# A mixer kernel on one core: the zero test of the attention scores moves from VectorE to two ScalarE passes

## The chip, the core and the metric

The kernel runs on one core of a Trainium2 chip. The metric is the device time of one launch in microseconds (us); lower is better. TensorE is PE in the rows below, VectorE is DVE, ScalarE is ACT, GpSimd is POOL, and SyncE is SP.

## What is computed

The reference is a chain of residual blocks over 16 sequences of 512 tokens of width 128: a mixture of experts, causal attention, the mixture again, and then two more mixtures around a state-space scan. Only the attention matters here:

```python
q = jnp.einsum('bse,ke->bsk', x, WQ)
k = jnp.einsum('bse,ke->bsk', x, WK)
v = jnp.einsum('bse,ve->bsv', x, WV)
scores = jnp.einsum('bsk,btk->bst', q, k) * SCALE
masked = jnp.where(jnp.tril(scores) == 0, -jnp.inf, scores)
attn = jax.nn.softmax(masked, axis=-1)
return jnp.einsum('bst,btv->bsv', attn, v)
```

A score is masked when it lies above the diagonal, and also when it is exactly zero.

## The kernel before, in words

The kernel is a row of stages with a barrier between them. The change is in `attention_stage`, whose tiles are named `att_...` in the rows. It keeps all tokens of all sequences in the resident tile `X`, and works through the 16 sequences s = 0 to 15 in order. Each sequence is cut into four row tiles i = 0 to 3 of 128 queries. Row tile i sees n = (i + 1) * 128 keys, so its scores are 128 x n, and there are 64 row tiles in all. `psS`, `hole`, `S`, `E`, `psE` and `PT` have two buffers each, taken in turn by row tiles.

For a row tile, PE writes the scores to `psS` and adds the causal triangle with a third matmul (L1046). DVE then makes `hole`, which is -1e30 where the score is exactly zero (L1248), adds it to the scores and takes the row maximum in one custom instruction (L1252), and scales the maximum into `ntop` (L1254, signal `topped`). ACT takes the exponential (L1178, signal `exped`). PE transposes it into `psE`, ACT copies that to `PT` (L1169), PE multiplies it with V into `psO`, and DVE divides and adds it to `X` (L1259, L1261; these two are `finish`).

Every engine has its own fixed program order, written out by hand, and the engines are tied by counting semaphores. PE runs one row tile ahead: its body for row tile i begins with the scores of i + 1. Between the row tiles stand the projections of the next sequence. ACT evicts K after row tile 1 (`att_KT`, L1156), then Q (`att_QT`, L1158), and V after row tile 2 (`att_V`, L1162). After that it normalizes the sequence after next (`att_xn`, L1147, four instructions), and evicts its transpose after row tile 3 (`att_xnT`, L1152).

The stage also routes its output to the experts of the next stage, for a pair of sequences at a time, and for one at a time at the end (s = 12 to 15). These are the tiles `att_r_...`. ACT normalizes them (`att_r_xn`, L246), PE transposes and multiplies, ACT evicts (`att_r_xnT`, L326) and takes an exponential (`att_r_prob`, L407), DVE picks the experts and writes the row numbers `att_r_idx` (L451), and POOL scatters the rows with one indirect DMA for 128 rows (L471). `att_r_xn` is a ring of two, so a group's normalized rows wait for the scatters of the group two before.

On DVE small pieces of routing and statistics work are woven into the gaps. `small.under(part)` runs one step of them at each point where `part` yields, and `chain.link` yields once after it has issued its instruction.

Of the kernel before, what the change touches and what calls it, by code (L numbers as in the profile page):

```python
# [15 lines left out]
ALU = mybir.AluOpType  # L16
ACT = mybir.ActivationFunctionType
AX = mybir.AxisListType

P = 128  # L20
# [24 lines left out]
EPS = 1e-5  # L45
NEG = -1e30
SCALE = D ** -0.5
INNER, STATES, RANK, TAPS = 256, 16, 64, 4
DT = INNER // P
PAD = 2 * (TAPS - 1)  # L50
# [714 lines left out]
def load_stage(nc, k, x, here, consts, l0_bg, gate_w, gamma, beta):  # L765


    with Stage(nc, "load") as st:
        loaded, zeroed, cleared = map(st.sem, ("loaded", "zeroed", "cleared"))
        empty = st.sb("empty", [P, SPREAD * ROW])  # L770
        token_i, slot_i = st.sb("token_i", [P, TILES], I32), st.sb("slot_i", [P, SPREAD], I32)
        raw = st.sb("raw", [P, 3 * P])
        counted = st.sem("counted")
        block = st.block()

        @block.gpsimd
        def _(pool):
            nc.gpsimd.iota(token_i[:, :], pattern=[[TOPK * P, TILES]], base=0, channel_multiplier=TOPK)
            nc.gpsimd.iota(slot_i[:, :], pattern=[[1, SPREAD]], base=0, channel_multiplier=SPREAD).then_inc(counted, 1)

        @block.sync
        def _(sp):
            wide = lambda v: v.rearrange("(a e) -> a e", a=1)
            for dst, src in ((raw[:, :], consts[:, P:4 * P]), (k.ident[:, :], consts[:, 0:P]), (k.small[:, :], consts[:, 36 * P:]),
                             (k.bg[:, :], wide(l0_bg).to_broadcast([P, EXPERTS])), (k.gamma[:, :], gamma.rearrange("(p a) -> p a", a=1)),
                             (k.beta[:, :], beta.rearrange("(p a) -> p a", a=1)), (k.gate_w[:, 0, :], gate_w[0]), (k.gate_w[:, 1, :], gate_w[1])):
                sp.dma_start(dst, src).then_inc(loaded, 16)
            for s in range(2):
                load_rows(sp, k, x, here, s)
            sp.wait_ge(loaded, 8 * 16)  # L790

        @block.scalar
        def _(act):
            act.wait_ge(cleared, 1)
            act.dma_start(k.xslots[DUMP:DUMP + BLOCK, :].rearrange("(p r) d -> p (r d)", p=P), empty[:, :]).then_inc(zeroed, 16)
            act.wait_ge(zeroed, 16)

        @block.vector
        def _(dve):
            nc.vector.memset(k.ones[:, :], 1.0)  # L800
            clear_rows(nc, empty[:, :]).then_inc(cleared, 1)
            dve.wait_ge(counted, 1)
            nc.vector.tensor_copy(k.token[:, :], token_i[:, :])
            nc.vector.tensor_copy(k.slot[:, :], slot_i[:, :])
            dve.wait_ge(loaded, 8 * 16)
            nc.vector.tensor_copy(k.before[:, :], raw[:, 0:P])
            nc.vector.tensor_copy(k.causal[:, :], raw[:, P:2 * P])
            nc.vector.tensor_copy(k.ident_bf[:, :], raw[:, 2 * P:3 * P])


# [150 lines left out]
def attention_stage(nc, k, wqkv, source):  # L961


    with Stage(nc, "att") as st:
        sem, sb, pb = st.sem, st.sb, st.pb
        w_ready, linked, normed, flipped, turned, q_summed, k_summed, v_summed, qk_ready, v_ready = map(
            sem, ("w_ready", "linked", "normed", "flipped", "turned", "q_summed", "k_summed", "v_summed", "qk_ready", "v_ready"))
        scored, topped, exped, p_flipped, p_turned, summed, added, holed, cleared = map(
            sem, ("scored", "topped", "exped", "p_flipped", "p_turned", "summed", "added", "holed", "cleared"))
        W = sb("W", [P, 3, P])  # L970
        xn = sb("xn", [P, 4, D])
        xnT = sb("xnT", [P, SEQ])
        QT, KT = sb("QT", [P, 2, SEQ]), sb("KT", [P, 2, SEQ])
        V = sb("V", [P, 2, 4, D])
        hole, S, E, PT = (sb(n, [P, 2, SEQ]) for n in ("hole", "S", "E", "PT"))
        top, ntop, total, inv = (sb(n, [P, SEQ_TILES]) for n in ("top", "ntop", "total", "inv"))
        empty = sb("empty", [P, SPREAD * ROW])
        psT = pb("psT", [P, SEQ])
        psQ, psO = pb("psQ", [P, SEQ]), pb("psO", [P, D])
        psS, psE = pb("psS", [P, 2, SEQ]), pb("psE", [P, 2, SEQ])  # L980
# [11 lines left out]
        there = lambda s: 0 <= s < BATCH  # L992
        block = st.block()
        ST = SEQ_TILES
# [144 lines left out]
        def _(act):  # L1139
# [10 lines left out]
            def turn_rows(s):  # L1150
                act.wait_ge(flipped, s + 1)
                nc.scalar.activation(xnT[:, :], psT[:, :], ACT.Copy).then_inc(turned, 1)  # L1152

            def project_qk(s, b):
                act.wait_ge(k_summed, s + 1)
                nc.scalar.activation(KT[:, b, :], psT[:, :], ACT.Copy).then_inc(qk_ready, 1)  # L1156
                act.wait_ge(q_summed, s + 1)
                nc.scalar.activation(QT[:, b, :], psQ[:, :], ACT.Copy).then_inc(qk_ready, 1)  # L1158

            def project_v(s, b):  # L1160
                act.wait_ge(v_summed, s + 1)
                nc.scalar.activation(V[:, b, :, :], psQ[:, :].rearrange("p (a d) -> p a d", a=4), ACT.Copy).then_inc(v_ready, 1)  # L1162

            def turn_p(s, i):
                t, n = s * ST + i, (i + 1) * P
# [5 lines left out]
            def body(s, b):  # L1171
                due, fresh = ends.get(s - 2), ends.get(s - 1)
                for i in range(ST):
                    t, n = s * ST + i, (i + 1) * P
                    act.wait_ge(topped, t + 1)
                    if t > 1:
                        act.wait_ge(p_flipped, t - 1)
                    nc.scalar.activation(E[:, i % 2, 0:n], S[:, i % 2, 0:n], ACT.Exp, bias=ntop[:, i:i + 1], scale=SCALE,  # L1178
                                         accum_out=total[:, i:i + 1]).then_inc(exped, 1)
                    if i > 0:  # L1180
                        turn_p(s, i - 1)
# [33 lines left out]
            N.act_root(nc, act, 1)  # L1215
            normal(1)
            turn_rows(1)
            for s in range(BATCH):
                body(s, s % 2)
            s, b, g = BATCH - 1, 1, len(pairs) - 1  # L1220
# [9 lines left out]
        def _(dve):  # L1230
            chain = Chain(dve, linked)
# [11 lines left out]

            def mask(s, i):
                t, n, h = s * ST + i, (i + 1) * P, i % 2
                dve.wait_ge(scored, t + 1)

                yield from chain.link(nc.vector.tensor_scalar(hole[:, h, 0:n], psS[:, h, 0:n], 0.0, NEG, ALU.is_equal, ALU.mult))  # L1248
                if t > 1:
                    dve.wait_ge(exped, t - 1)  # L1250
                dve.sem_inc(holed, 1)
                yield from chain.link(nc.vector.tensor_tensor_reduce(out=S[:, h, 0:n], in0=psS[:, h, 0:n], in1=hole[:, h, 0:n], scale=1.0, scalar=3.0 * NEG,  # L1252
                                                                     op0=ALU.add, op1=ALU.max, accum_out=top[:, i:i + 1]))
                nc.vector.tensor_scalar(ntop[:, i:i + 1], top[:, i:i + 1], -SCALE, None, ALU.mult).then_inc(topped, 1)  # L1254

            def finish(s, i):
                t = s * ST + i
# [62 lines left out]
            s, g = BATCH - 1, len(pairs) - 1  # L1320
# [637 lines left out]
```

## Time and profile before

| | |
|---|---|
| time of 3 runs, median (lowest to highest) | 3136.72 us (3132.16 to 3138.05) |
| the profiled execution: own time | 3140.43 us |
| the profiled execution: span of its instructions | 3138.6 us |
| PE busy | 2462.0 us (78%) |
| DVE busy | 2072.7 us (66%) |
| ACT busy | 1591.6 us (51%) |
| POOL busy | 1698.8 us (54%) |

The profiled execution's own time lies 1.8 us above its span. The busy shares are averages over all stages with different limits, so they say little about the attention stage. That stage stands between about 484 and 798 us of the span.

### The profile page before, as it was taken

How to read it: one execution, taken by the hardware profiler on the slowest of the kernel's cores; microseconds unless marked ns; L12 is line 12 of the kernel's file. 1: busy time of each engine (PE TensorE's matmuls, PEld its weight loads, DVE VectorE, ACT ScalarE, POOL GpSimd, SP SyncE). 2: the span in 40 equal slices, each digit the busy share in tenths (PEclk: the TensorE clock that was granted, in tenths of full speed). 3: DMA queues.
4: the chain of work that ended last, by engine and by line, in shares of the span. 5: the costliest groups of instructions: out<-in, count | busy, mean ns of one | idle time of the engine just before them, and what ended most of it. 6: DMA issues, size and time to landing. Idle time of an engine off the chain costs nothing. (4 is left out here: it accounts for less than half of the span.)

```text
span 3138.6 us, 49074 instructions
## 1 busy us (share of the span) xinstructions
PE 2462.0 (78%) x12952; PEld 1742.6 (56%) x12952; DVE 2072.7 (66%) x6083; ACT 1591.6 (51%) x3093; POOL 1698.8 (54%) x1349
## 2 busy tenths in 40 slices
PE   4239995884799754399978888888988898759991
PEld 4239994663799633399933333333433343349991
DVE  6414445775344455155539999999999999955553
ACT  3115554672455443255546666656666666425550
POOL 5745550455355347555515567666666667645551
PEclk9999998996899966699989999999999999879995
DMA  9147771211677532477724344434334344237775
GB/s 329 53 131 229 226 224 58 69 53 41 205 228 226 159 99 78 131 229 226 216 75 142 129 134 143 140 124 136 136 124 133 135 136 145 102 114 228 226 227 170
DMA packets 268819, 479.26 MB, mean 153 GB/s; under 512 B 37453, under 2 KB 181803, under 8 KB 268560
## 3 DMA queue, kind: packets, MB, share of 16 engines
q1 hardware_dynamic: 225280, 405.41, 42.4%
q0 software_dynamic: 34816, 68.00, 6.0%
q10 hardware_dynamic: 8592, 4.33, 0.5%
q8 instruction: 54, 0.88, 0.1%
q14 instruction: 77, 0.63, 0.1%
HBM read 383.22 MB, written 98.54 MB: 153 GB/s over the span
## 5 line engine op out<-in xcount | busy, mean ns | idle before, releaser
L1731 POOL TENSOR_TENSOR ssm_HC<-ssm_H,ssm_BC 128x1024 f32<-128x1024 f32 x255 | 599.4, 2351 | 416.3 <-DVE ssm_psX L1801 329.3
L1492 PE MATMUL ssm_psY<-ssm_HC,ident 128*128 128x512 f32 x1020 | 516.9, 634 | 94.0 <-POOL ssm_HC L1731 93.8
L1650 ACT ACTIVATE ssm_dA<-ssm_delta,A 128x511 f32<-128x511 f32 x512 | 332.9, 710 | 194.0 <-DVE ssm_H L1810 133.9
L1492 PEld LDWEIGHTS ssm_psY<-ssm_HC,ident 128*128 128x128 f32 x1020 | 192.6, 198 | 363.6 <-issue 201.4
L1808 DVE TENSOR_TENSOR_SCAN ssm_H<-ssm_dA,ssm_psX 128x512 f32<-128x512 f32 x256 | 309.7, 1210 | 0.0
L1810 DVE TENSOR_TENSOR_SCAN ssm_H<-ssm_dA,ssm_psX 128x512 f32<-128x512 f32 x256 | 305.4, 1193 | 0.0
L471 POOL DMA_INDIRECT xslots<-att_r_xn,att_r_idx x128 | 128.3, 1002 | 176.6 <-DVE att_r_idx L451 138.5
L877 POOL DMA_INDIRECT b_back<-b_yr,b_to_row x144 | 139.8, 971 | 151.2 <-DVE b_yr L952 129.3
L877 POOL DMA_INDIRECT a_back<-a_yr,a_to_row x144 | 139.8, 971 | 150.4 <-DVE a_yr L952 128.4
L877 POOL DMA_INDIRECT d_back<-d_yr,d_to_row x144 | 139.8, 971 | 147.9 <-DVE d_yr L952 126.0
L877 POOL DMA_INDIRECT c_back<-c_yr,c_to_row x144 | 139.8, 971 | 143.1 <-DVE c_yr L952 119.3
L921 ACT ACTIVATE b_H<-b_psH,b_W 128x256 f32<-128x256 f32 x288 | 127.4, 473 | 125.6 <-PE b_psH L898 125.6
L921 ACT ACTIVATE d_H<-d_psH,d_W 128x256 f32<-128x256 f32 x288 | 127.4, 473 | 125.3 <-PE d_psH L898 125.3
L921 ACT ACTIVATE a_H<-a_psH,a_W 128x256 f32<-128x256 f32 x288 | 127.4, 473 | 124.4 <-PE a_psH L898 124.4
L921 ACT ACTIVATE c_H<-c_psH,c_W 128x256 f32<-128x256 f32 x288 | 127.4, 473 | 123.9 <-PE c_psH L898 123.9
L921 ACT ACT_TABLE_LOAD x72 | 92.4, 1283 | 183.4 <-PEq L162 182.2
L471 POOL DMA_INDIRECT xslots<-ssm_r_xn,ssm_r_idx x128 | 160.1, 1251 | 34.1 <-issue 23.7
L1801 DVE TENSOR_TENSOR ssm_psX<-ssm_ux,ssm_BC 128x512 f32<-128x512 f32 x256 | 176.4, 689 | 0.0
L471 POOL DMA_INDIRECT xslots<-to_c_r_xn,to_c_r_idx x128 | 125.7, 982 | 91.1 <-DVE to_c_r_idx L451 51.1
L1796 DVE TENSOR_TENSOR ssm_psX<-ssm_ux,ssm_BC 128x512 f32<-128x512 f32 x256 | 174.0, 680 | 0.6
L1428 PE MATMUL ssm_psA<-ssm_hT,Wtap 128*128 128x512 f32 x360 | 165.4, 603 | 5.4 <-ACT ssm_hT L1586 5.1
L471 POOL DMA_INDIRECT xslots<-to_a_r_xn,to_a_r_idx x128 | 125.5, 981 | 66.4 <-issue 41.0
(566 smaller groups left out, 5817.6 us busy)
## 6 DMA issues: line engine op xcount, KB each, us to landing
ssm_BC<-bc_rows SPq DMA_DIRECT2D x128, 1024.0 KB, 5.5
a_W<-in_l_pack SPq DMA_DIRECT2D x72, 514.0 KB, 3.4
b_W<-in_l_pack SPq DMA_DIRECT2D x72, 514.0 KB, 3.3
c_W<-in_l_pack SPq DMA_DIRECT2D x72, 514.0 KB, 3.4
d_W<-in_l_pack SPq DMA_DIRECT2D x72, 514.0 KB, 3.4
a_xs<-xslots SPq DMA_DIRECT2D x72, 131.0 KB
b_xs<-xslots SPq DMA_DIRECT2D x72, 131.0 KB
c_xs<-xslots SPq DMA_DIRECT2D x72, 131.0 KB
```

What stands on the lines that cost most here:

```text
L471: pool.indirect_dma_start(out=self.k.xslots[:, :], out_offset=bass.IndirectOffsetOnAxis(ap=self.ids(s, b)[:, i:i + 1].bitcast(U32), axis=0 ...
L877: pool.indirect_dma_start(out=target[:, :], out_offset=bass.IndirectOffsetOnAxis(ap=to_row[:, q, s:s + 1].bitcast(U32), axis=0), in_=yr[:, ...
L921: nc.scalar.activation(H[:, b, f, :], psH[:, f, 0:BLOCK], gelu, bias=W[:, q, HIDDEN + FT * D + f:HIDDEN + FT * D + f + 1]).then_inc(h_read ...
L1428: last = nc.tensor.matmul(out, Wtap[:, c, t, dt * P:(dt + 1) * P], hT[:, PAD - back:PAD - back + SEQ], start=(t == 0), stop=(t == TAPS - 1))
L1492: last = nc.tensor.matmul(psY[:, dt, :], k.ident[:, :], HC[:, n % RP, dt, :], start=(n == 0), stop=(n == NB - 1))
L1650: last = nc.scalar.activation(dA[:, n % RA, dt, 1:], delta[:, b, dt, 1:], ACT.Exp, scale=A[:, dt, n:n + 1])
L1731: nc.gpsimd.tensor_tensor(HC[:, n % RP, :, :], H[:, n % RH, :, :], BC[:, n // CHUNK % SLOTS, 1, n % CHUNK:n % CHUNK + 1, :].to_broadcast([ ...
L1796: nc.vector.tensor_tensor(psX[:, 0, :], ux[:, 0, :], BC[:, c % SLOTS, 0, n % CHUNK, :], ALU.mult).then_inc(dBx_half, 1)
L1801: nc.vector.tensor_tensor(psX[:, 1, :], ux[:, 1, :], BC[:, c % SLOTS, 0, n % CHUNK, :], ALU.mult).then_inc(dBx_done, 1)
L1808: nc.vector.tensor_tensor_scan(H[:, n % RH, 0, :], dA[:, n % RA, 0, :], psX[:, 0, :], 0.0, ALU.mult, ALU.add).then_inc(h_half, 1)
L1810: nc.vector.tensor_tensor_scan(H[:, n % RH, 1, :], dA[:, n % RA, 1, :], psX[:, 1, :], 0.0, ALU.mult, ALU.add).then_inc(h_ready, 1)
```

## The change

`hole` is now made by ACT, in two passes: `|score * 1e36|`, and then `max(0, 1 - that)`, which is 1 for an exact zero and 0 otherwise. For this the queries carry a factor of -2^-50, so that a hole of 1 is large against any score. DVE waits for `holed` in place of `scored`, and its custom instruction negates the sum. The exponential and `ntop` have the factor taken back in their scales. The causal constant is 1 in place of -1e30; it is made once, in the first stage.

ACT makes the holes of row tile i + 1 ahead of the exponential of row tile i. DVE's `mask` has one `chain.link` less, so it steps the woven work once less for each row tile.

```diff
+SHRINK = 2.0 ** -50
...
-            nc.vector.tensor_copy(k.causal[:, :], raw[:, P:2 * P])
+            nc.vector.tensor_scalar(k.causal[:, :], raw[:, P:2 * P], 1.0 / NEG, None, ALU.mult)
...
-                nc.scalar.activation(QT[:, b, :], psQ[:, :], ACT.Copy).then_inc(qk_ready, 1)
+                nc.scalar.activation(QT[:, b, :], psQ[:, :], ACT.Copy, scale=-SHRINK).then_inc(qk_ready, 1)
...
+            def holes(s, i):
+
+                t, n, h = s * ST + i, (i + 1) * P, i % 2
+                act.wait_ge(scored, t + 1)
+                nc.scalar.activation(hole[:, h, 0:n], psS[:, h, 0:n], ACT.Abs, scale=1e36).then_inc(distant, 1)
+                act.wait_ge(distant, t + 1)
+                nc.scalar.activation(hole[:, h, 0:n], hole[:, h, 0:n], ACT.Relu, scale=-1.0, bias=1.0).then_inc(holed, 1)
...
                 for i in range(ST):
                     t, n = s * ST + i, (i + 1) * P
+                    if t > 0:
+                        act.wait_ge(topped, t)
+                    if i + 1 < ST:
+                        holes(s, i + 1)
+                    elif there(s + 1):
+                        holes(s + 1, 0)
                     act.wait_ge(topped, t + 1)
                     if t > 1:
                         act.wait_ge(p_flipped, t - 1)
-                    nc.scalar.activation(E[:, i % 2, 0:n], S[:, i % 2, 0:n], ACT.Exp, bias=ntop[:, i:i + 1], scale=SCALE,
+                    nc.scalar.activation(E[:, i % 2, 0:n], S[:, i % 2, 0:n], ACT.Exp, bias=ntop[:, i:i + 1], scale=SCALE / SHRINK,
                                          accum_out=total[:, i:i + 1]).then_inc(exped, 1)
...
+            holes(0, 0)
...
-                dve.wait_ge(scored, t + 1)
-
-                yield from chain.link(nc.vector.tensor_scalar(hole[:, h, 0:n], psS[:, h, 0:n], 0.0, NEG, ALU.is_equal, ALU.mult))
+                dve.wait_ge(holed, t + 1)
                 if t > 1:
                     dve.wait_ge(exped, t - 1)
-                dve.sem_inc(holed, 1)
-                yield from chain.link(nc.vector.tensor_tensor_reduce(out=S[:, h, 0:n], in0=psS[:, h, 0:n], in1=hole[:, h, 0:n], scale=1.0, scalar=3.0 * NEG,
+                dve.sem_inc(begun, 1)
+                yield from chain.link(nc.vector.tensor_tensor_reduce(out=S[:, h, 0:n], in0=psS[:, h, 0:n], in1=hole[:, h, 0:n], scale=-1.0, scalar=3.0 * NEG,
                                                                      op0=ALU.add, op1=ALU.max, accum_out=top[:, i:i + 1]))
-                nc.vector.tensor_scalar(ntop[:, i:i + 1], top[:, i:i + 1], -SCALE, None, ALU.mult).then_inc(topped, 1)
+                nc.vector.tensor_scalar(ntop[:, i:i + 1], top[:, i:i + 1], -SCALE / SHRINK, None, ALU.mult).then_inc(topped, 1)
```

ACT's program in the middle of an odd sequence, from the exponential of row tile 1 on. Before:

```order
L1178 ACTIVATE att_E,att_total<-att_S,att_ntop 128x256
L1169 ACTIVATE att_PT<-att_psE 128x128
L326 ACTIVATE att_r_xnT<-att_psQ 128x512
L1156 ACTIVATE att_KT<-att_psT 128x512
L1158 ACTIVATE att_QT<-att_psQ 128x512
L1178 ACTIVATE att_E,att_total<-att_S,att_ntop 128x384
```

And of the change, the same place:

```order
L1169 ACTIVATE att_hole<-att_psS 128x384
L1171 ACTIVATE att_hole<-att_hole 128x384
L1193 ACTIVATE att_E,att_total<-att_S,att_ntop 128x256
L1178 ACTIVATE att_PT<-att_psE 128x128
L327 ACTIVATE att_r_xnT<-att_psQ 128x512
L1157 ACTIVATE att_KT<-att_psT 128x512
L1159 ACTIVATE att_QT<-att_psQ 128x512
L1169 ACTIVATE att_hole<-att_psS 128x512
L1171 ACTIVATE att_hole<-att_hole 128x512
L1193 ACTIVATE att_E,att_total<-att_S,att_ntop 128x384
```

Two instructions have come in ahead of every exponential, and nothing else has moved. The number of table loads in ACT's program is the same, 72.

DVE's program in an even sequence, between the scores of row tile 2 and those of row tile 3 (128x512). `att_n_shift` ends the statistics that ACT's `att_xn` waits for, and `att_r_pos` waits for PE's routing matmuls. Before:

```order
L1252 ISA att_S,att_top<-att_psS,att_hole 128x384
L1252 ISA att_top 128x1
L234 SCALAR_TENSOR_TENSOR att_n_rstd<-att_n_newton,att_n_root 128x8
L211 TENSOR_SCALAR att_r_mean<-att_r_mean 128x8
L212 SCALAR_TENSOR_TENSOR att_r_odd<-att_r_odd 128x8
L1254 TENSOR_SCALAR att_ntop<-att_top 128x1
L239 SCALAR_TENSOR_TENSOR att_n_shift<-att_n_mean,att_n_rstd 128x8
L213 SCALAR_TENSOR_TENSOR att_r_var<-att_r_var,att_r_odd 128x8
L447 TENSOR_TENSOR att_r_pos<-att_psR,att_r_run 128x128
```

And of the change, the same place:

```order
L1266 ISA att_S,att_top<-att_psS,att_hole 128x384
L1266 ISA att_top 128x1
L234 TENSOR_TENSOR att_n_newton<-att_n_newton,att_n_shifted 128x8
L209 TENSOR_TENSOR att_r_mean<-att_r_stats 128x8
L210 TENSOR_TENSOR att_r_var<-att_r_stats 128x8
L211 TENSOR_TENSOR att_r_odd<-att_r_stats 128x8
L1268 TENSOR_SCALAR att_ntop<-att_top 128x1
L235 SCALAR_TENSOR_TENSOR att_n_rstd<-att_n_newton,att_n_root 128x8
L212 TENSOR_SCALAR att_r_mean<-att_r_mean 128x8
L213 SCALAR_TENSOR_TENSOR att_r_odd<-att_r_odd 128x8
L448 TENSOR_TENSOR att_r_pos<-att_psR,att_r_run 128x128
L240 SCALAR_TENSOR_TENSOR att_n_shift<-att_n_mean,att_n_rstd 128x8
```

With one yield less, the woven statistics are one step behind: `att_n_shift` stood ahead of `att_r_pos` and now stands behind it.

## Rows read from the trace of the kernel before

**Rows 1.** Stretches (start:end, length): engines' busy us (instructions), PEclk, DMA share, GB/s.

```profile
510.00:546.39 36.39, 29.52 (x176) 22.82 (x177) 27.26 (x123) 21.46 (x64) 0.00 (x0) 0.92 0.19 59
631.92:659.99 28.07, 23.73 (x196) 19.08 (x196) 22.00 (x117) 20.06 (x56) 16.44 (x17) 1.00 0.26 77
```

**Rows 2.** Who waited for whom, 500 to 760: total, times, longest.

```profile
ACT att_E L1178 <- DVE att_ntop L1254: 51.5, 37, 4.4
```

**Rows 3.** ACT's timeline, one pair: start, length, [idle before <-releaser].

```profile
631.92 0.72 ACT L1178 ACTIVATE att_E<-att_S,att_ntop 128x512 f32<-128x512 f32 x1 [0.83 <-DVE att_ntop L1254]
...
635.02 0.39 ACT L1178 ACTIVATE att_E<-att_S,att_ntop 128x128 f32<-128x128 f32 x1
...
636.43 1.64 ACT L246 ACTIVATE att_r_xn<-X,att_r_shift,att_r_rstd 128x128 f32<-128x128 f32 x4
...
642.38 0.60 ACT L1158 ACTIVATE att_QT<-att_psQ 128x512 f32<-128x512 f32 x1 [1.16 <-PE att_psQ L1028]
643.15 0.61 ACT L1178 ACTIVATE att_E<-att_S,att_ntop 128x384 f32<-128x384 f32 x1 [0.17 <-DVE att_ntop L1254]
...
648.04 0.72 ACT L1178 ACTIVATE att_E<-att_S,att_ntop 128x512 f32<-128x512 f32 x1 [1.12 <-DVE att_ntop L1254]
...
650.67 0.20 ACT L223 ACTIVATE att_n_root<-att_n_shifted 128x8 f32<-128x8 f32 x1
650.90 0.21 ACT L225 ACTIVATE att_n_root<-att_n_root 128x8 f32<-128x8 f32 x1
...
655.83 0.61 ACT L1178 ACTIVATE att_E<-att_S,att_ntop 128x384 f32<-128x384 f32 x1 [1.49 <-DVE att_ntop L1254]
...
659.99 0.72 ACT L1178 ACTIVATE att_E<-att_S,att_ntop 128x512 f32<-128x512 f32 x1 [0.83 <-DVE att_ntop L1254]
```

**Rows 4.** DVE's and PE's timelines in that pair.

```profile
658.17 0.68 DVE L1248 TENSOR_SCALAR att_hole<-att_psS 128x512 f32<-128x512 f32 x1
...
659.07 0.69 DVE L1252 CUSTOM_DVE_ANT_0 att_S<-att_psS,att_hole 128x512 f32<-128x512 f32 x1
...
642.18 0.81 PE L1044 MATMUL att_psS<-att_KT,att_QT 128*128 128x384 f32 x2
...
643.04 0.22 PE L1046 MATMUL att_psS<-causal,ident_bf 128*128 128x128 bf16 x1
```

**Rows 5.** ACT groups by shape, 480 to 790: busy, mean ns | idle before.

```profile
L246 ACT ACTIVATE att_r_xn<-X,att_r_shift,att_r_rstd 128x128 f32<-128x128 f32 x64 | 26.3, 484 | 9.8 <-DMA xslots<-att_r_xn,att_r_idx 6.9 <-DVE att_r_shift L239 2.9
...
L1169 ACT ACTIVATE att_PT<-att_psE 128x512 f32<-128x512 f32 x16 | 9.3, 580 | 0.0
...
L1178 ACT ACTIVATE att_E<-att_S,att_ntop 128x128 f32<-128x128 f32 x16 | 6.3, 395 | 0.4
...
L1169 ACT ACTIVATE att_PT<-att_psE 128x128 f32<-128x128 f32 x16 | 4.1, 257 | 0.5 <-PE att_psE L1052 0.5
```

**Rows 6.** The same view of the scan stage.

```profile
L1632 ACT ACTIVATE ssm_pre<-ssm_psA,col 128x512 f32<-128x512 f32 x31 | 21.2, 682 | 23.3 <-PE ssm_psA L1466 23.3
...
L1637 ACT ACTIVATE ssm_rest<-ssm_pre 128x1024 f32<-128x1024 f32 x16 | 16.9, 1057 | 0.5
```

**Rows 7.** ACT's timeline at the stage's start.

```profile
525.04 0.39 ACT L1178 ACTIVATE att_E<-att_S,att_ntop 128x128 f32<-128x128 f32 x1
...
529.89 0.51 ACT L1178 ACTIVATE att_E<-att_S,att_ntop 128x256 f32<-128x256 f32 x1 [3.89 <-DVE att_ntop L1254]
...
535.15 0.71 ACT L1178 ACTIVATE att_E<-att_S,att_ntop 128x512 f32<-128x512 f32 x1
...
546.39 0.71 ACT L1178 ACTIVATE att_E<-att_S,att_ntop 128x512 f32<-128x512 f32 x1
```

**Rows 8.** ACT's and POOL's timelines at its end.

```profile
710.66 1.65 ACT L246 ACTIVATE att_r_xn<-X,att_r_shift,att_r_rstd 128x128 f32<-128x128 f32 x4 [0.52 <-DMA xslots<-att_r_xn,att_r_idx]
...
733.19 1.65 ACT L246 ACTIVATE att_r_xn<-X,att_r_shift,att_r_rstd 128x128 f32<-128x128 f32 x4 [6.38 <-DMA xslots<-att_r_xn,att_r_idx]
...
689.13 0.97 POOL L471 DMA_INDIRECT xslots<-att_r_xn,att_r_idx  x1 [8.82 <-DVE att_r_idx L451]
```

More of the change, by code:

```diff
@@ L967, in attention_stage @@
             sem, ("w_ready", "linked", "normed", "flipped", "turned", "q_summed", "k_summed", "v_summed", "qk_ready", "v_ready"))
-        scored, topped, exped, p_flipped, p_turned, summed, added, holed, cleared = map(
-            sem, ("scored", "topped", "exped", "p_flipped", "p_turned", "summed", "added", "holed", "cleared"))
+        scored, topped, exped, distant, begun, p_flipped, p_turned, summed, added, holed, cleared = map(
+            sem, ("scored", "topped", "exped", "distant", "begun", "p_flipped", "p_turned", "summed", "added", "holed", "cleared"))
         W = sb("W", [P, 3, P])
```

## Prediction

> **What bounds the kernel now.** The change lies in the attention stage alone, so the page's shares say nothing, and I read the stage by stretches first. From 631.92 to 659.99, one pair of sequences, PE is busy 23.7 of 28.1 us, DVE 22.0 and ACT 20.1 [rows 1]. No engine is full: they take turns in waiting. The list of waits says for whom: ACT waited 51.5 us, 37 times, for DVE's `ntop` before the exponential [rows 2]. That looks like room on ACT, and like a VectorE on the path. So the question is where on ACT's timeline this room is, since ACT's order is fixed. It is in lumps: 0.83 and 1.12 us ahead of row tile 3, 1.49 ahead of row tile 2 of the even sequence [rows 3]. From 631.92 to the end of `att_r_xn` at 638.07 ACT has next to none: the exponential at 635.02 starts without a wait [rows 3]. At the stage's end ACT waits for scatters: the wait of 6.38 us at 733.19 [rows 8].
>
> **What is removed.** 64 DVE passes. Of a 512-wide row tile the pass starts at 658.17 and the custom instruction at 659.07 [rows 4], so its `ntop` can come 0.90 us earlier, if the holes are there.
>
> **What is added: the price of a pass.** Neither pass is in the trace in its form. Abs from PSUM: below, the copy `att_PT`, 0.257 us for 128 and 0.580 for 512; above, `ssm_pre` L1632, which also reads a bias column, 0.682 for 512 [rows 5, 6]. I take 0.27 to 0.59, near the copy, since the new pass has no column. Relu from SBUF: L1637 is an affine with constants only, 1.057 us for 1024 [rows 6]; the copies' slope is 0.108 us per 128 [rows 5], which gives 0.63 for 512 and 0.30 for 128. Above it lies the exponential, 0.395 for 128, which reads a column [rows 5]. The second pass waits for the first on the same engine, like the pair at 650.67 and 650.90: a start 0.03 us after the end of the first [rows 3]. An instruction that doesn't wait overlaps its forerunner by 0.10: the four of `att_r_xn` at 636.43 last 1.64 together, and one lasts 0.484 [rows 3, 5]. Two passes thus take 0.51, 0.72, 0.93 and 1.16 us for row tiles 0 to 3: **3.32 us a sequence**. By the bounds it is 3.06 (two copies) to 4.03 (both with a column).
>
> The Trainium skill, page "ScalarE: Activation LUTs", section "What ACT_TABLE_LOAD costs", gives 186 ns + 0.833 ns an element for constants, 93 ns more for each column and 93 ns of overlap. The rows above bear it out (0.63 here, 0.61 by the rule); by it an estimate is 3.37 us a sequence, 0.6 us more in the whole sum.
>
> **Where the passes land: a pair.** I go along ACT's order from the exponential of row tile 3 at 631.92 to the one at 659.99 [rows 3], with each start at the later of ACT's and its giver's.
> - Odd half. ACT's 3.1 us to 635.02 stay. Then come passes for row tile 1 (0.72) with nothing to hide in, so the second half of `att_r_xn` ends 0.72 late, at 638.8. Passes for row tile 2 (0.93) take the place of a wait. PE transposes that `att_r_xn` and has K and Q behind it, so Q's scores come 0.75 late too. QT starts at 643.1 (before 642.38), still after a wait of 1.15. The passes for row tile 3 need their scores, which PE needs 1.08 us for after Q (642.18 to 643.26, [rows 4]): a wait of 0.42 behind QT's 0.5, then 1.16. The exponential of row tile 2 goes from 643.15 to 645.2. V, `att_r_prob` and `att_xn` follow 1.3 to 1.5 late. DVE's routing waits for `att_r_prob`, so of its 0.90 gained, 0.6 are lost: `ntop` at 648.5. ACT gets there at 648.2 and, after 0.51 of passes, starts row tile 3 at 648.7, where it was 648.04.
> - Even half. 0.72 + 0.93 + 1.16 + 0.51 us of passes. The waits they could fill are those for `ntop`, 0.88, 1.49 and 0.83, and what is left are short waits for PE (0.12, 0.25, 0.40), since K, Q and the scores of row tile 3 now start from an ACT that is late with `att_PT`.
> - `att_n_shift` now stands behind `att_r_pos` in DVE's program, so `att_xn` waits another 0.33 for PE's routing matmuls.
>
> Sum: start to start ACT's own work in the pair is 19.4 us (its busy 20.06 [rows 1] less the overlaps). Add 6.64 of passes and the waits left: 0.57 for K, 1.15 and 0.42, and 0.12 + 0.25 + 0.40 + 0.33, together 3.2. 19.4 + 6.6 + 3.2 = 29.2 us where it was 28.07: **+1.15 us a pair**. ACT is now what the pair lasts; what is late next is PE, behind `att_PT` and the exponential.
>
> **The start.** Sequences 0 to 2 carry no routing on ACT, and it is busy 21.5 of 36.4 us [rows 1]. The first holes wait for `att_xnT`, so the exponential at 525.04 comes 3.9 late. The wait of 3.89 at 529.89, for DVE's sums and statistics [rows 7], swallows 3 of it, for DVE's new order puts this `ntop` only 0.35 later. From there ACT is full: the exponential of row tile 3 at 535.15 comes 3.15 late and the one at 546.39 **4.0** late (a sequence of 11.24 us becomes 12.1: some 10.6 of work and passes and 1.2 to 1.5 of waits for K, Q and scores).
>
> **The end.** From the scatters that begin at 689.13 on [rows 8], 16 DMAs and the free ring buffer set `att_r_xn` at 710.66, and the next 16 that at 733.19. Lateness that ACT adds in between fits into the waits of 0.52 and 6.38. Five pairs lie between 546.39 and there: 5 x 1.15 = 5.75. After 733.19 DVE is the late one again: the passes cost 0.45, the last removed pass gives back 0.90, so -0.45.
>
> The causal constant, the scale on QT and the scaled `ntop` are the same instructions with other numbers: nothing. Total: 4.0 + 5.75 - 0.45 = **+9.3 us**. The profiled execution took 3140.43 us (span 3138.6, 1.8 around it), so its like would take 3149.7; it lies 3.7 above the median of the runs, and against 3136.72 the forecast is **3146.0 us**, +0.30%.
>
> **The rivals.**
> - *Hidden.* ACT's 51.5 us of waiting [rows 2] take up nearly all of 16 x 3.3 = 53 us, and the rest is noise: 3137 us. For it: the waits are of the right size and ahead of the right instruction. Against: they lie in the wrong half, and some turn into waits for PE.
> - *The path through DVE gets shorter (faster).* If the passes fit, row tile 3's `ntop` comes 0.90 earlier in both halves, and PE's next scores and `att_xnT` with it: 5 x 1.8 = 9, so 3128 us. It decides whether ACT has 0.5 us free ahead of row tile 3 after its `att_xn`. In the trace it idles there 1.12 and 0.83 [rows 3]; but V comes late by the passes of row tile 3, which eat that.
> - *Dearer passes or a lower clock (slower still).* With the upper prices a sequence has 0.7 us more, over 13 sequences 9: 3155 us. Likewise the granted clock: 1.00 with PE busy 85% of a pair, 0.92 at the start with 81% [rows 1], so there it fell from the 2.4 GHz level part of the time. A pair of 29.2 us has PE at 81%. If that brings 0.92, PE's 23.7 us become 25.8, at most 2 us a pair on top, so 3156 us.
>
> **How the numbers follow.** I give my sum 0.62, hidden 0.20, faster 0.08 and dearer 0.10. The sum's own range is 3140 to 3152: lower prices take 13 x 0.26 = 3.4 off, and waits left out come on top. A measurement of this kernel tells about 0.2%, 6.3 us, from no change; my sum lies 3 us over that, so I count 0.54 of its 0.62 as slower. Slower 0.64, same 0.20 + 0.08 = 0.28, faster 0.08. The range takes in "hidden" and most of the dearer case: 3136 to 3157.
>
> **What would show it.** Right: a pair lasts 29 to 29.5 us, ACT busy 26 or more of them; its waits for `ntop` fall from 51.5 to under 15 us, while those for K, Q and scores grow; the exponential that was at 546.39 is 4 us later; a 512-wide Abs takes 0.57 to 0.62 and a Relu 0.61 to 0.65. The stage's length up to the next stage's first matmul grows by some 9 us, and the other stages keep theirs. Wrong: passes of 0.7 us; a pair of 28 us with ACT still waiting for `ntop` (then PE or DVE was the bound and ACT had room); or a start that costs nothing, since the wait of 3.89 us there swallows all.

## The result, and the profile after

The changed kernel took 3142.07 us (median of 20 runs, 3138.2 to 3148.98), the kernel before on the same chip 3135.77 (20 runs, 3130.06 to 3141.29). The ratio is 1.0023, with a 95% interval of 1.0017 to 1.0029: slower by 0.23%, 6.3 us. A second comparison on another chip gave 3144.19 against 3135.07, ratio 1.0030 [1.0018, 1.0042], 9.1 us. The profiled execution after has a time of its own of 3141.97 us and a span of 3140.2.

The spans of the two profiled executions differ by 1.6 us only, so the first thing to do is to cut them at the stage. I cut from the table load that opens the attention stage on ACT (488.31 before, 489.09 after) to the first matmul of the next stage (800.86 and 811.07). Kernel before, both parts by windows:

```profile
488.31:800.86 312.55, 206.21 (x1536) 165.38 (x1537) 202.40 (x1040) 164.83 (x450) 128.28 (x128) 0.83 0.20 60
800.86:3138.60 2337.74, 1931.00 (x9016) 1274.16 (x9016) 1649.66 (x4086) 1234.83 (x2234) 1304.73 (x943) 0.91 0.50 157
```

And after:

```profile
489.09:811.07 321.98, 213.75 (x1536) 169.62 (x1536) 175.02 (x976) 212.24 (x578) 125.41 (x128) 0.83 0.20 58
811.07:3140.20 2329.13, 1920.64 (x9016) 1268.80 (x9016) 1649.32 (x4086) 1234.75 (x2234) 1304.89 (x943) 0.92 0.51 157
```

The stage grew by 9.43 us. The rest has the same instructions and was 8.6 us shorter, with PE busy 10 us less at a slightly higher granted clock: the profiled execution of before happened to lie 4.7 us above its own median. Only the stage tells of the change. In it ACT has 128 instructions and 47.4 us more, DVE 64 instructions and 27.4 us less.

Stretches of the stage after, the start and then a pair; they answer to [rows 1]:

```profile
512.50:552.48 39.98, 33.22 (x180) 24.86 (x179) 23.89 (x119) 31.29 (x88) 0.00 (x0) 0.85 0.20 53
581.69:610.90 29.21, 24.07 (x198) 19.15 (x197) 18.52 (x108) 25.80 (x73) 15.62 (x17) 1.00 0.25 74
```

ACT's busy time in a pair went from 20.1 to 25.8 us, a little under the 26 that the prediction named as its sign, and the pair from 28.07 to 29.21. DVE is now busy 18.5. The list of waits, 500 to 770, against [rows 2]:

```profile
DVE X L1275 <- PE att_psO L1065: 31.4, 27, 6.9
...
DVE att_S L1266 <- ACT att_hole L1171: 17.1, 15, 4.2
ACT att_QT L1159 <- PE att_psQ L1029: 10.1, 15, 1.2
ACT att_hole L1169 <- PE att_psS L1047: 8.8, 17, 2.0
ACT att_E L1193 <- DVE att_ntop L1268: 8.2, 3, 3.2
ACT att_KT L1157 <- PE att_psT L1024: 7.5, 14, 2.2
```

The roles are turned round: ACT's 51.5 us of waiting for `ntop` are down to 8.2, all three of them at the stage's end, and DVE waits for ACT's holes and for PE's `psO`, which needs ACT's exponentials and `PT`. The waits for K and Q did not grow, as the prediction had it: they were 9.6 and 9.9 before. New are those for the scores, 8.8. ACT's timeline of the pair answers to [rows 3]:

```profile
581.69 0.71 ACT L1193 ACTIVATE att_E<-att_S,att_ntop 128x512 f32<-128x512 f32 x1
...
591.05 0.60 ACT L1157 ACTIVATE att_KT<-att_psT 128x512 f32<-128x512 f32 x1 [0.50 <-PE att_psT L1024]
592.80 0.60 ACT L1159 ACTIVATE att_QT<-att_psQ 128x512 f32<-128x512 f32 x1 [1.15 <-PE att_psQ L1029]
593.78 0.60 ACT L1169 ACTIVATE att_hole<-att_psS 128x512 f32<-128x512 f32 x1 [0.39 <-PE att_psS L1047]
594.41 0.63 ACT L1171 ACTIVATE att_hole<-att_hole 128x512 f32<-128x512 f32 x1
...
598.48 0.71 ACT L1193 ACTIVATE att_E<-att_S,att_ntop 128x512 f32<-128x512 f32 x1
...
603.83 0.60 ACT L1157 ACTIVATE att_KT<-att_psT 128x512 f32<-128x512 f32 x1 [0.18 <-PE att_psT L1024]
604.69 0.60 ACT L1159 ACTIVATE att_QT<-att_psQ 128x512 f32<-128x512 f32 x1 [0.26 <-PE att_psQ L1029]
605.67 0.60 ACT L1169 ACTIVATE att_hole<-att_psS 128x512 f32<-128x512 f32 x1 [0.39 <-PE att_psS L1047]
...
608.50 1.65 ACT L1148 ACTIVATE att_xn<-X,att_n_shift,att_n_rstd 128x128 f32<-128x128 f32 x4 [0.22 <-DVE att_n_shift L240]
...
610.90 0.71 ACT L1193 ACTIVATE att_E<-att_S,att_ntop 128x512 f32<-128x512 f32 x1
```

These seven rows with a bracket are all of ACT's waits in 29.21 us, 3.09 us together. The odd half takes 16.79 us where it took 16.12, the even half 12.42 where it took 11.95. The price of a pass, in the view of [rows 5]:

```profile
L1171 ACT ACTIVATE att_hole<-att_hole 128x512 f32<-128x512 f32 x16 | 10.1, 630 | 0.5
L1169 ACT ACTIVATE att_hole<-att_psS 128x512 f32<-128x512 f32 x16 | 9.6, 598 | 7.4 <-PE att_psS L1047 7.4
...
L1171 ACT ACTIVATE att_hole<-att_hole 128x128 f32<-128x128 f32 x16 | 5.0, 310 | 0.5
L1169 ACT ACTIVATE att_hole<-att_psS 128x128 f32<-128x128 f32 x16 | 4.2, 261 | 0.0
```

The end of the stage, against [rows 8]:

```profile
743.69 1.65 ACT L247 ACTIVATE att_r_xn<-X,att_r_shift,att_r_rstd 128x128 f32<-128x128 f32 x4 [6.20 <-DMA xslots<-att_r_xn,att_r_idx]
```

From the table load this `att_r_xn` is at 254.60 where it was at 244.88: 9.72 us late, of which 9.43 reach the next stage.

### The profile page after: what moved, and what is told of

Read it like the earlier page. It is cut to its first block and busy times, and to the rows that moved or that the text cites. A ratio compares the mean times of both kernels' runs of the same rounds, so it can differ in the third digit from the quotient of the medians.

```text
span 3140.2 us, 49200 instructions
## 1 busy us (share of the span) xinstructions
PE 2460.2 (78%) x12952; PEld 1742.2 (55%) x12952; DVE 2044.7 (65%) x6019; ACT 1638.9 (52%) x3221; POOL 1696.0 (54%) x1349
```

## The experiments

All medians below stand beside runs of the kernel before on the same chip. "A pair" is the time from the 512-wide exponential of one even sequence to that of the next even one; the pair with routing begins with s = 2. The experiments ran on three chips.

**The first chip was no good for this.** On it the kernel before took 3278.32 us, 4.5% more than elsewhere, and every kernel's pair was near 40 us. Most of it lies in the attention stage: in the version with the relief alone it takes 415.33 us there and 303.35 on the second chip, 112 of the 154 us between the two medians. DVE's and ACT's timelines of that version there, `e1_relief`:

```profile
621.87 0.60 ACT L326 ACTIVATE att_r_xnT<-att_psQ 128x512 f32<-128x512 f32 x1 [5.23 <-remote]
...
633.11 0.23 DVE L399 TENSOR_TENSOR att_r_L<-att_psR,bg 128x64 f32<-128x64 f32 x1 [12.81 <-remote]
633.15 0.60 ACT L1158 ACTIVATE att_QT<-att_psQ 128x512 f32<-128x512 f32 x1 [6.45 <-DMA a_xs<-xslots]
```

ACT stands for 5 to 6 us ahead of an eviction, and the transfer named, of another stage's tile, is nothing that the eviction depends on. Such waits come in every pair but the first, and the stage's start is 40 us longer too. They swallow or add microseconds at will, so I read from this chip only the first pair, and put all four of its questions again on the others. Why that chip stands there is left open.

### Only the relief: DVE's pass removed, nothing added

The kernel before without DVE's zero test. `hole` is cleared once, so exact zeros aren't masked. With the line goes its step of woven work, so DVE has the order of the change here too, `att_n_shift` behind `att_r_pos`.

```diff
+            chain(nc.vector.memset(hole[:, :, :], 0.0))
...
-                yield from chain.link(nc.vector.tensor_scalar(hole[:, h, 0:n], psS[:, h, 0:n], 0.0, NEG, ALU.is_equal, ALU.mult))
```

> The kernel before without DVE's zero pass and without any ACT pass: the hole tile is zeroed once, so only the causal triangle masks and exact zeros are not looked for. It measures what the relief of DVE is worth by itself. Theory A (ACT's passes cost what DVE's relief gives and more): row tile 3's ntop comes 0.9 us earlier in both halves of a pair, so a pair of 28.07 us takes 26.3 to 27.3, and the kernel is 5 to 11 us faster than before. Rival B (DVE's pass was never on the path): a pair of 28.0 us, the time of before within 2 us.

> The kernel before without DVE's zero pass and without an ACT pass, as in the first call (the hole tile is zeroed once, so only the causal triangle masks), to see its time where the stage has no stalls. In the first call its first pair took 26.88 us where before takes 28.06, but the later ones 38 to 42 with stalls in them. Theory A: without stalls 27.0 us a pair and 6 to 11 us faster than before. Rival B: within 2 us of before.

Measured: on the first chip 3280.68 against 3278.32, ratio 1.0011 [0.9996, 1.0027], with a first pair of 26.88. On the second 3126.39 against 3135.07, ratio 0.9965 [0.9951, 0.9978], 8.7 us faster; the stage takes 303.35 us. A pair there:

```profile
600.40:627.00 26.60, 22.95 (x198) 19.02 (x197) 18.26 (x107) 19.92 (x57) 15.87 (x16) 1.00 0.27 82
```

So DVE's path did set part of the time: 1.47 us a pair, with the changed order in it. The pair of 27.0 that was expected is undercut by 0.4. The change had that to gain.

### Only the cost: two more passes on ACT, DVE's kept

The passes read `KT` and write a tile that nobody uses; they stand and wait where the change's do.

```diff
+            def holes(s, i):
+
+                t, n, h = s * ST + i, (i + 1) * P, i % 2
+                act.wait_ge(scored, t + 1)
+                nc.scalar.activation(extra[:, h, 0:n], KT[:, s % 2, 0:n], ACT.Abs, scale=1e36).then_inc(distant, 1)
+                act.wait_ge(distant, t + 1)
+                nc.scalar.activation(extra[:, h, 0:n], extra[:, h, 0:n], ACT.Relu, scale=-1.0, bias=1.0).then_inc(passed, 1)
```

> The kernel before with its DVE zero pass kept, and ACT's two passes added at the places of the change, with the same wait for the scores, but reading the K tile from SBUF and writing a tile that nobody reads. It measures the passes' cost without DVE's relief and without DVE waiting for ACT. Theory A: ACT's own time is the cost, so a pair takes 29.2 to 30.2 us and the kernel is 9 to 16 us slower than before. Rival B (the passes fit into ACT's waits, and the cost of the change is DVE waiting for the holes): a pair of 28.1 to 28.5 us, at most 3 us slower than before.

> The kernel before with two more ScalarE passes per row tile, of the same lengths and at the same places as in the change, but with KT for a source and an unused tile for a target; DVE's zero test stays, and its order too. Theory (the cost of the change is ScalarE's work, its relief is DVE's pass gone): both costs and no relief, a pair of 30.8 us and 14 to 22 us slower than before, so 8 to 14 us slower than the change. Rival (the wait of DVE on ACT's holes is what costs, and ScalarE's own work is hidden in its 51.5 us of waiting): a pair of 28.1 to 28.6 and at most 3 us slower than before.

Measured: on the first chip ratio 1.0053 [1.0038, 1.0068], first pair 30.77. On the third 3151.11 against 3134.6, ratio 1.0050 [1.0035, 1.0064], 16.5 us slower, the stage 328.04 us, pairs of 30.1 to 30.5 where 30.8 was expected. The first, with a granted clock of 0.94, is below; the one pair at 1.00 takes 30.13.

```profile
552.41:582.50 30.09, 25.43 (x196) 20.01 (x194) 21.68 (x114) 26.19 (x73) 0.20 (x1) 0.94 0.13 36
```

ACT's passes alone cost 16.5 us, although ACT waited 51.5 us before. With the relief of 8.7 they make 7.8, and the change measured 6.3 and 9.1. But the intervals of these two ratios are some 4 us wide to either side, so that sum can't exclude a third term, and the stage in the profiles shows one. There the relief gives 9.20 us and the passes cost 15.49, together 6.3, where the change costs 9.43 and 9.95. In a pair at a clock of 1.00 the two make 2.06 less 1.47, 0.59 us, and the change costs 1.14. So on top of ACT's passes DVE's relief gives back less than by itself, 0.92 us (30.13 to 29.21). What takes the rest, DVE's waits for the holes or an ACT that has no room for an earlier `ntop`, no run separates. The row for `KT` shows something by the way, shown at the end.

### Half the cost: one pass on ACT

The changed kernel with one pass per row tile. It leaves out the test for zero, so its holes aren't holes.

```diff
-                nc.scalar.activation(hole[:, h, 0:n], psS[:, h, 0:n], ACT.Abs, scale=1e36).then_inc(distant, 1)
-                act.wait_ge(distant, t + 1)
-                nc.scalar.activation(hole[:, h, 0:n], hole[:, h, 0:n], ACT.Relu, scale=-1.0, bias=1.0).then_inc(holed, 1)
+                nc.scalar.activation(hole[:, h, 0:n], psS[:, h, 0:n], ACT.Relu, scale=1e-30).then_inc(holed, 1)
```

> The changed kernel with only one ACT pass for a row tile (a Relu of the scores times 1e-30, so the hole tile is practically zero and only the causal triangle masks). It halves the suspected cost. Theory A (ACT's passes set the pair): 3.3 us a pair less of ACT work, of which the waits for PE and DVE take back some: a pair of 27.0 to 27.8 us, 7 to 11 us faster than the change and 0 to 4 faster than before. Rival B (the order of waits, holes before the exponential, is what costs and not the passes' length): a pair of 28.7 us or more, at most 3 us faster than the change.

> The changed kernel with one ScalarE pass in place of the two (the Relu of the scores times 1e-30 straight from PSUM; it leaves out the test for zero, so its holes aren't holes). The order on DVE is that of the change, and the passes for row tiles 0 to 3 take 0.31 to 0.63 us, half of the two. Again on a chip where the attention stage doesn't stand still. Theory (the length of ACT's work in a pair makes the change slower, and what DVE is relieved of comes out as soon as ACT's work is short enough): a pair of 27.1 to 27.3 us (before 28.07), 0 to 6 us faster than before. Rival (DVE's order, with att_n_shift behind att_r_pos, costs time whatever ACT does): a pair of 28.3 or more, slower than before.

Measured: on the first chip ratio 1.0049 [1.0033, 1.0064], which is worth little there; its first pair is 27.15. On the third 3127.35 against 3134.6, ratio 0.9982 [0.9973, 0.9991]: faster by 7.2 us, a little more than the 0 to 6 expected; its stage is 5.0 us shorter than before. All five pairs take 27.13 us. Windows, and ACT's timeline in a pair:

```profile
657.13:684.26 27.13, 23.16 (x198) 19.07 (x197) 18.35 (x108) 22.25 (x64) 16.07 (x16) 1.00 0.13 41
```

```profile
638.91 0.60 ACT L1157 ACTIVATE att_KT<-att_psT 128x512 f32<-128x512 f32 x1 [1.06 <-PE att_psT L1024]
...
650.40 0.60 ACT L1157 ACTIVATE att_KT<-att_psT 128x512 f32<-128x512 f32 x1 [0.64 <-PE att_psT L1024]
...
655.08 1.65 ACT L1148 ACTIVATE att_xn<-X,att_n_shift,att_n_rstd 128x128 f32<-128x128 f32 x4 [0.89 <-DVE att_n_shift L240]
```

The pair shrinks by 2.08 us for 3.55 us less of ACT's busy time. So ACT's second pass is what turns the gain of DVE's relief into a loss. At half the price ACT no longer sets the pair alone: its waits for PE and for `att_n_shift` make 4.77 us in place of 3.09. The first pass costs little, 0.53 us against the 26.60 with the relief alone.

### The order on DVE: one more step of woven work

The changed kernel with `yield` once more in `mask`, ahead of the wait for `holed`, so that `att_n_shift` stands ahead of `att_r_pos` again.

```diff
+                yield
                 dve.wait_ge(holed, t + 1)
```

> The changed kernel with one more yield in mask, ahead of its wait, so that the woven work steps as often as before and att_n_shift stands ahead of att_r_pos again. Theory A with its 0.33 us a pair for att_n_shift: 28.9 us a pair, 1.5 to 2.5 us faster than the change. Rival B (the step is free, or the statistics that now stand between the custom instruction and ntop cost as much): the time of the change within 1 us, a pair of 29.2.

> The changed kernel with one more step of woven work per row tile, so that DVE's order is again that of before (att_n_shift ahead of att_r_pos). Theory by the prediction's term (att_xn waits 0.33 us a pair longer by that order): a pair of 28.9 us, 1.5 us less in the stage. Rival (on the full ACT this wait is swallowed by another): a pair of 29.2 to 29.4, and the time that of the change, 3142 to 3144 where before is 3136, within 1 us.

Measured: on the first chip ratio 1.0059 [1.0043, 1.0075]. On the third 3142.92 against 3134.6, ratio 1.0027 [1.0018, 1.0037], the stage 321.52 us. The wait of 0.22 ahead of `att_xn` is gone:

```profile
695.71 1.64 ACT L1148 ACTIVATE att_xn<-X,att_n_shift,att_n_rstd 128x128 f32<-128x128 f32 x4
```

This pair, from 669.09 to 698.10, takes 29.01 us: its even half 12.10 in place of 12.42, its odd half 16.91 in place of 16.79. The other pairs take 29.36, 29.76 (with a granted clock of 0.94), 29.14 and 29.08, so against 29.21 the gain is 0.2 us in the best pair and none in the first. The stage is 0.5 to 1 us shorter (321.98 and 322.50 in the two profiles of the changed kernel), but these have one and two pairs at a lower clock, and the whole can't be told from the changed kernel. So the order costs at most 0.2 us a pair on the full ACT, not the 0.33 of the theory.

### Passes only where ACT waited

Three kernels give ACT a part of the row tiles and leave DVE the others, with the new scales everywhere. The condition is `by_act`.

```diff
+        by_act = lambda s, i: s % 2 == 0 and i == 3
...
+                if by_act(s, i):
+                    dve.wait_ge(holed, held(s, i))
+                else:
+                    dve.wait_ge(scored, t + 1)
+                    yield from chain.link(nc.vector.tensor_scalar(hole[:, h, 0:n], psS[:, h, 0:n], 0.0, 1.0, ALU.is_equal, ALU.mult))
```

Row tile 3 of the even sequences:

> A mixture: ACT makes the holes only for row tile 3 of even sequences, where the kernel before had ACT waiting 1.49 us ahead of the exponential of row tile 2; DVE makes all others, as before. Theory A (what counts is whether a pass finds ACT idle): the passes of 1.16 us fit, ntop of that row tile comes up to 0.9 us earlier, a pair of 27.2 to 28.0 us, and 2 to 6 us faster than before. Rival B (any ACT pass delays): a pair of 28.5 us or more and 1 to 4 us slower than before.

Row tile 3 of all sequences, `i == 3`:

> The same with row tile 3 of every sequence on ACT. In the odd half the passes wait for scores that PE finishes only after Q's, and they stand ahead of V, whose lateness reaches DVE's routing. Theory A: that half gives back what the even half gains, a pair of 27.8 to 28.6 us, and -3 to +2 us against before. Rival B: a pair of 29 us or more, 5 us slower than before.

Row tiles 2 and 3 of the even sequences, `s % 2 == 0 and i > 1`:

> ScalarE makes the holes of row tiles 2 and 3 of the even sequences alone, where it waited 1.49 and 0.83 us for DVE's ntop; DVE makes the other 48. Against the version with row tile 3 of the even sequences alone, which had a pair of 27.17 and was 3.5 us faster than before. Theory (a pass is free only where ACT waits for DVE): the 0.93 us for row tile 2 fit into the 0.88 us ahead of its forerunner's exponential, so a pair of 27.1 to 27.3 and 2 to 6 us faster than before. Rival (ACT is already the bound in that version, so any pass adds its length): a pair of 28.0 us, equal to before within 2 us.

And the changed kernel again, beside the first two of them:

> The changed kernel again, on another chip than the first result, to have its trace beside the experiments. Theory A: a pair of 29.2 us as before, and +0.2 to +0.3% against the kernel before, if this chip has no stalls of its own. Rival C (the chip on which the first four experiments ran holds engines back while they wait for nothing in the program, and there more instructions cost more than their time): where such stalls show, +0.4 to +0.6%.

| holes made by ACT | us against before | ratio | load to E(2,3) | pair | stage |
|---|---|---|---|---|---|
| none (before, profiled) | | | 58.08 | 28.07 | 312.55 |
| even, row tile 3 | 3131.61 against 3135.07 | 0.9986 [0.9977, 0.9995] | 59.97 | 27.17 | 309.36 |
| all, row tile 3 | 3133.04 against 3135.07 | 0.9988 [0.9979, 0.9997] | 60.30 | 27.13 | 309.28 |
| even, row tiles 2 and 3 | 3133.47 against 3134.6 | 0.9997 [0.9988, 1.0006] | 60.72 | 27.52 | 312.08 |
| all (the change, again) | 3144.19 against 3135.07 | 1.0030 [1.0018, 1.0042] | 63.09 | 29.22 | 322.50 |

E(2,3) is the exponential of row tile 3 of sequence 2. The pair is the undisturbed one of the five: the second version has one of 28.65 besides, the last one of 30.07, one of 30.08 and one of 29.34. In the row of before the stage has two pairs of 29.39 at a clock of 0.94 in it, 2.6 us above five pairs of 28.07.

ACT's timeline of the first version, in the even half, shows how a pass goes for nothing; compare the wait of 1.49 at 655.83 in [rows 3]:

```profile
654.38 0.60 ACT L1171 ACTIVATE att_hole<-att_psS 128x512 f32<-128x512 f32 x1 [0.38 <-PE att_psS L1049]
655.01 0.63 ACT L1173 ACTIVATE att_hole<-att_hole 128x512 f32<-128x512 f32 x1
655.55 0.60 ACT L1194 ACTIVATE att_E<-att_S,att_ntop 128x384 f32<-128x384 f32 x1
...
656.89 1.64 ACT L1150 ACTIVATE att_xn<-X,att_n_shift,att_n_rstd 128x128 f32<-128x128 f32 x4
...
658.77 0.71 ACT L1194 ACTIVATE att_E<-att_S,att_ntop 128x512 f32<-128x512 f32 x1
```

The two passes fill the wait, and the exponential of row tile 3 finds its `ntop` ready. The pair gains 0.90 us, the length by which DVE's `ntop` comes earlier [rows 4]. The stage gains less than five times that. In this profile its start is 1.89 us longer, 1.18 of it before any pass stands in ACT's way, and of the 5.22 us that row tile 3 of sequence 12 comes earlier, counted from the load, only 3.19 reach the next stage.

The second version misses both of its expectations, 27.8 to 28.6 and 29: with passes in the odd sequences as well the pair is 27.13. So the passes of an odd row tile 3 are free too. ACT's timeline of the second version, in the odd half:

```profile
592.34 0.58 ACT L1165 ACTIVATE att_V<-att_psQ 128x512 f32<-128x512 f32 x1
...
594.80 0.72 ACT L1194 ACTIVATE att_E<-att_S,att_ntop 128x512 f32<-128x512 f32 x1 [0.21 <-DVE att_ntop L1274]
```

In the first version, where DVE makes these holes, ACT waits 0.54 us ahead of `att_V` (617.13) and 1.12 ahead of this exponential (620.53). The passes fill both waits, and the half takes 15.92 us in place of 16.11. The even half gives 0.14 of that back, so nothing more is gained.

The third version should have kept 27.17 if the 0.93 us for row tile 2 fit into the wait of 0.88 there. They do: the exponential behind them starts 3.95 us after that of row tile 3 (620.50 to 624.45), and 3.94 in the first version (647.70 to 651.64). But the pair is 27.52. Its timeline shows where most of the 0.35 lies:

```profile
623.50 0.49 ACT L1171 ACTIVATE att_hole<-att_psS 128x384 f32<-128x384 f32 x1
...
624.45 0.49 ACT L1194 ACTIVATE att_E<-att_S,att_ntop 128x256 f32<-128x256 f32 x1
...
630.02 1.65 ACT L1150 ACTIVATE att_xn<-X,att_n_shift,att_n_rstd 128x128 f32<-128x128 f32 x4 [0.23 <-DVE att_n_shift L240]
```

`att_xn` starts 9.52 us after that exponential of row tile 3, in the first version 9.19: 0.33 us later. It waits for `att_n_shift`, which lost a step on DVE when the pass of row tile 2 went. In its trace `att_r_pos` waits 1.77 us for PE and starts at 629.56, and `att_n_shift` comes behind it at 629.84; in the first version `att_n_shift` starts ahead of it, at 655.38. So the theory's 27.3 and the rival's 28.0 both failed for the pair: ACT has the room, and the order of the woven work takes 0.33 of it back. The whole time, 1.1 us below before and within its noise, missed the theory's 2 to 6 and is what the rival said.

The first version beats both kernels: 3131.61 us, 3.5 faster than before, by the interval 1.6 to 7.2. With the woven step put back where a pass goes, row tile 2 might be had for nothing too; that wasn't run.

## Why the prediction was right

Forecast 3146.0, 0.30% slower; measured 3142.07 and, the second time, 3144.19, 0.23 and 0.30% slower than the kernel before beside them. The two chips and the profiled executions give +6.3, +9.1 and +9.43 in the stage for the forecast +9.3. Of the 3.9 us between 3146.0 and 3142.07 the kernel before has 0.95: 3136.72 in the three runs of the forecast, 3135.77 in twenty. The agreement in the stage is better than its parts.

**The price of a pass** was right: 0.598 and 0.630 us for 512, 0.261 and 0.310 for 128, inside or beside the ranges taken from the copy and the affine [rows 5, 6]. In the pair above the two passes take 0.51, 0.72, 0.94 and 1.17 us, 3.34 a sequence for the forecast 3.32.

**The pair** was right to 0.01 us, 29.21 for 29.2, and so by its parts: the odd half 16.79 for 16.8 (648.7 less 631.92), the even half 12.42, waits of 3.09 us for 3.2, the one for `att_n_shift` 0.22 for 0.33. This is the term that a walk along ACT's order gets and a look at the 51.5 us of waiting doesn't. The experiment with the cost alone shows that the passes weren't hidden; the versions with row tile 3's passes alone show that there they are, in both halves.

But five pairs cost 4.19 us and not 5.75 in the profiled executions. That isn't the mechanism: before had two pairs of 29.39 with a granted clock of 0.94, and after one of 30.23 with 0.89 and one of 29.33 at 1.00. Without them five pairs would cost 5.7. Before, the pair from 659.99 on:

```profile
659.99:689.38 29.39, 25.12 (x196) 20.64 (x196) 22.02 (x117) 20.17 (x56) 16.00 (x17) 0.94 0.12 38
```

**The start was under-sized**: 5.31 us from load to E(2,3), forecast 4.0. The lateness, each from its own load, against the forecast:

| | forecast | measured |
|---|---|---|
| `att_V` of sequence 0, ahead of all passes | none named | 0.96 |
| exponential that was at 525.04, E(1,0) | 3.9 | 5.12 |
| exponential that was at 529.89, E(1,1) | 0.9 | 2.27 |
| E(1,3) | 3.15 | 4.46 |
| E(2,3) | 4.0 | 5.31 |

The mis-sized terms are the first two of that sum: "the exponential at 525.04 comes 3.9 late", which measured 5.12, and "DVE's new order puts this `ntop` only 0.35 later", which measured 2.27. The wait of 3.89 swallowed 2.85 for the 3 forecast, and from E(1,1) on each step is right: 2.19 more for 2.25, then 0.85 for 0.85. At E(1,1) both engines are late together. ACT's second pass ends at 532.83 and DVE's `ntop` at 532.90, so neither alone is the cause:

```profile
532.31 0.52 ACT L1171 ACTIVATE att_hole<-att_hole 128x384 f32<-128x384 f32 x1
...
532.94 0.51 ACT L1193 ACTIVATE att_E<-att_S,att_ntop 128x256 f32<-128x256 f32 x1
```

```profile
528.14 0.35 DVE L1275 SCALAR_TENSOR_TENSOR X<-att_psO,att_inv,X 128x128 f32<-128x128 f32 x1 [1.71 <-PE att_psO L1065]
...
530.95 0.35 DVE L1275 SCALAR_TENSOR_TENSOR X<-att_psO,att_inv,X 128x128 f32<-128x128 f32 x1 [0.17 <-PE att_psO L1065]
...
532.76 0.14 DVE L1268 TENSOR_SCALAR att_ntop<-att_top 128x1 f32<-128x1 f32 x1
```

Ahead of this `ntop` on DVE stand the last divisions of sequence 0. They wait for PE's `psO` (1.71, 0.17), and that for ACT's late exponentials and `PT`. I let DVE run its own course there; ACT's lateness also goes round by DVE.

Part of the 5.31 can be chance. The V projection of sequence 0 met another clock. Windows and ACT's row for `att_V`, before and then after:

```profile
505.00:511.00 6.00, 2.11 (x15) 1.87 (x15) 1.91 (x9) 3.14 (x8) 0.00 (x0) 0.78 0.00 0
```

```profile
506.89 0.60 ACT L1162 ACTIVATE att_V<-att_psQ 128x512 f32<-128x512 f32 x1 [1.25 <-PE att_psQ L1033]
```

```profile
506.00:512.00 6.00, 2.61 (x11) 2.23 (x11) 0.65 (x4) 2.99 (x8) 0.00 (x0) 0.50 0.00 0
```

```profile
508.63 0.60 ACT L1163 ACTIVATE att_V<-att_psQ 128x512 f32<-128x512 f32 x1 [2.16 <-PE att_psQ L1034]
```

The granted clock is at 0.50 throughout in after, the level of 1.2 GHz, and has risen from it part of the time in before. ACT waits 0.91 us longer for it. Of the profiles from the last two chips, two have the short wait (`e2_passes_2`, `e3_step_2`) and six the long one, the relief alone among them, whose ACT program is that of before. So it doesn't come from the passes. How much of the missing 1.3 us it explains stays open. In `e3_step_2`, with the short wait and all the passes, the start took 63.08 less 58.08 = 5.0 us more; but that version has the other order on DVE, its `ntop` comes later still, and ACT waits 1.77 us for it. The changed kernel's second profile has the long wait and 5.01.

**The end** was off by a little. The `att_r_xn` that was at 733.19 came 9.72 us late, forecast 4.0 + 5.75 = 9.75, and from there to the next stage 0.29 came back, forecast 0.45. E(12,3) was 9.50 late (210.57 against 201.07 from the load), so from there 0.07 came back in all.

So the total, 5.31 + 4.19 - 0.07 = 9.43, hits 4.0 + 5.75 - 0.45 = 9.3 since a start forecast 1.3 too low met pairs forecast 1.6 too high, and the latter by the clock's chance in before. That the two cancel is luck.

**The rivals.** "Hidden" fell: the pair isn't 28, and the passes alone cost 16.5 us. But the reason given against it, that ACT's waits "lie in the wrong half", holds only in part: the passes of row tile 3 found room in the odd half as well. What the change pays for comes with row tiles 0 to 2: with row tile 3's holes alone on ACT the pair is 27.13, with all of them there 29.21, although DVE is then relieved of all its passes. "Faster by DVE" was right about what DVE's path holds (8.7 us by the relief alone, where I had 9), but its condition isn't met in the change: behind `att_xn` and the passes for row tile 0 the exponentials of row tile 3 start without a wait, at 598.48 and 610.90. "Dearer passes" fell by the rows above. Its other half, the clock, didn't come as it was put: with PE busy 24.07 of 29.21 us the granted clock was 1.00. Pairs at 0.89 or 0.94 came once in the first profile of the changed kernel and twice in the second, 0.7 to 1.0 us above their neighbours, but before had two of them as well.

## What to carry to other kernels

An engine's total of waiting is no room until each wait is set beside the instruction that would fill it: 51.5 us of waiting took up the passes of row tile 3 (free in both halves of a pair, 3.5 us gained with those of the even half) and not all of them (9.4 us lost in the stage). Two terms measured by themselves needn't add up either: here they made 6.3 us of these 9.4. Walk an engine's order with each start at the later of its own and its giver's, and follow the lateness through the other engines too, above all at a start, where they catch up with each other. When an instruction with a woven step is removed, look at what the missing step delays: here 0.33 us a pair in one version, and at most 0.2 where ACT was full. And cut two profiles at the stage before they are compared: the spans differed by 1.6 us where the stage differed by 9.4.

## What the runs showed of the hardware

An ACT pass over 128x512, Abs with a constant scale and an SBUF target, took 33 ns longer from SBUF than from PSUM. Groups by shape of `e2_passes_2`, the Abs that reads `KT` in SBUF, where the one that reads `psS` takes 598:

```profile
L1168 ACT ACTIVATE att_extra<-att_KT 128x512 f32<-128x512 f32 x16 | 10.1, 631 | 7.3 <-PE att_psS L1046 7.0 <-DVE att_ntop L1269 0.4
```

At 128 wide it is 296 from SBUF and 261 from PSUM. The Trainium skill, page "ScalarE: Activation LUTs", section "What ACT_TABLE_LOAD costs", gives 186 ns + 0.833 ns an element for a pass with constants. By it an estimate for 512 is 0.613 us, with no term for the source; the traces have 0.598 and 0.631 on either side of it.

The second thing is the first chip: the same program took 4.5% longer there, and in the attention stage ACT and DVE stood for 5 to 13 us at a time for which I found no dependence of the program. A ratio measured there said something other than on the two other chips (the one-pass version 0.49% slower there, 0.18% faster on the third).
